# Graph-network kernel on one core: the last two pairs of edge blocks, with dst rows spread earlier and their output vectors in other PSUM banks

## The reference

```python
h = maximum(layernorm(x), 0)                              # 12500 x 32
e = concatenate([h[src], h[dst], edge_attr], axis=-1)     # 400000 x 96
v = relu(e @ W1 + b1) @ W2 + b2                           # 96 -> 64 -> 32
out = x + maximum(segment_max(v, dst), h)
```

## Time and profile before

| | us |
|---|---|
| median of three runs | 3227.99 |
| lowest, highest | 3225.35, 3228.82 |
| the profiled execution, its own time | 3226.88 |
| its span in the trace | 3224.7 |
| TensorE busy | 3004.2 |
| GpSimd busy | 2415.8 |
| VectorE busy | 2190.4 |
| ScalarE busy | 2111.5 |

### The profile page before, as it was taken

The page is one execution under the profiler, slowest core; times in us unless marked ns, Lnnn a source line. Parts: engine busy times, 40 slices in busy tenths (PEclk is TensorE's granted clock), DMA queues, the critical chain, the costliest instruction groups (busy, mean ns, idle before and its releaser), DMA issues.

```text
span 3224.7 us, 56108 instructions
## 1 busy us (share of the span) xinstructions
PE 3004.2 (93%) x19600; PEld 2220.3 (69%) x19600; DVE 2190.4 (68%) x2400; ACT 2111.5 (65%) x2463; POOL 2415.8 (75%) x2547
## 2 busy tenths in 40 slices
PE   6999999999999999999999999999998998999910
PEld 4776677777777777777777777777776776777700
DVE  6221677777777777777777777777776776777643
ACT  2335677777777777777777777777776775777510
POOL 7777777777777777777777777777777777777756
PEclk9999999999999999999999999999999999999955
DMA  9930333333333333333333333333333323333221
GB/s 310 362 128 27 84 101 101 100 99 99 95 98 98 100 96 102 100 98 95 97 99 98 100 97 101 101 98 85 106 98 90 100 77 102 101 99 98 75 47 26
DMA packets 194363, 337.83 MB, mean 105 GB/s; under 512 B 74115, under 2 KB 118101, under 8 KB 193712
## 3 DMA queue, kind: packets, MB, share of 16 engines
q1 hardware_dynamic: 110520, 292.58, 26.5%
q0 software_dynamic: 81216, 41.73, 10.1%
q10 hardware_dynamic: 2482, 2.14, 0.2%
HBM read 227.85 MB, written 108.41 MB: 104 GB/s over the span
## 4 chain that ended last, share of the span: by engine, by line
PE 89%; POOL 3%; issue 3%; DMA 3%; DVE 2%; SPq 0%; ACT 0%; DVEq 0%; POOLq 0%; ACTq 0%
PE ps_rows L734 67%; PE ps_layers L713 4%; PE ps_layers L715 4%; PE ps_layers L748 3%; PE ps_layers L763 3%; PE ps_layers L772 3%; PE ps_layers L752 3%; POOL gathered_max L597 2%; PE ps_layers L758 2%; DMA picks<-picks_dram 1%; POOL src_in L524 1%; DVE onehot L969 1%; DMA gathered_max<-run_max,gather_ix 1%; DMA src_in<-h_dram,src_ix 0%; DMA dst_i<-in_dst_dram 0%
## 5 line engine op out<-in xcount | busy, mean ns | idle before, releaser
L524 POOL DMA_INDIRECT src_in<-h_dram,src_ix x2293 | 2166.4, 945 | 698.8 <-issue 635.4
L734 PE MATMUL ps_rows<-onehot,table 128*128 128x512 f32 x9800 | 2288.7, 393 | 22.1 <-DVE onehot L969 22.1
L734 PEld LDWEIGHTS ps_rows<-onehot,table 128*128 128x128 f32 x9800 | 1830.0, 188 | 496.6 <-issue 107.3
L665 ACT ACTIVATE onehot<-distance 128x1024 fp32r<-128x1024 bf16 x882 | 878.9, 1049 | 701.2 <-PE ps_rows L734 701.2
L660 ACT ACTIVATE distance<-picks,below_column 128x1024 bf16<-128x1024 int16 x882 | 954.7, 1136 | 36.8 <-DMA picks<-picks_dram 36.8
L969 DVE SCALAR_TENSOR_TENSOR onehot<-picks,column,ps_layers 128x1024 fp32r<-128x1024 int16 x392 | 493.0, 1278 | 365.3 <-PE ps_rows L734 345.9
L713 PE MATMUL ps_layers<-ea_t,rows_in 125*128 125x320 bf16 x980 | 269.0, 302 | 25.4 <-DVE rows_in L838 25.4
L1015 DVE STREAM_TRANSPOSE ps_layers<-rows_in 128x512 f32<-128x512 f32 x196 | 129.4, 705 | 221.2 <-ACT hid L651 191.5
L715 PE MATMUL ps_layers<-dst_t,rows_in 125*128 125x320 bf16 x980 | 268.9, 301 | 0.0
L651 ACT ACTIVATE hid<-ps_layers,b_col 128x512 f32<-128x512 f32 x392 | 234.1, 674 | 37.7 <-PE ps_layers L763 37.7
L1030 DVE TENSOR_TENSOR_SCAN max_t<-mask_in,max_t,ps_layers 128x512 f32<-128x512 bf16 x196 | 250.4, 1278 | 9.0 <-PE ps_layers L772 5.5
(11 more groups left out here) (106 smaller groups left out, 1049.3 us busy)
## 6 DMA issues: line engine op xcount, KB each, us to landing
picks<-picks_dram SPq DMA_DIRECT2D x98, 512.0 KB, 11.0
first_rows<-hid SPq DMA_DIRECT2D x100, 500.0 KB
rows_in<-in_edge_attr_dram SPq DMA_DIRECT2D x97, 512.0 KB
rows_in<-first_rows SPq DMA_DIRECT2D x97, 512.0 KB
run_max<-rows_in SPq DMA_DIRECT2D x96, 512.0 KB
src_in<-h_dram,src_ix POOLq DMA_INDIRECT x2293
mask_in<-mask_dram SPq DMA_DIRECT2D x97, 256.0 KB
h_dram<-h_sb ACTq DMA_DIRECT2D x1, 1568.0 KB, 6.6
```

The source lines that it names most:

```text
L524: pool.indirect_dma_start(out=src_in[:, slot, g, r, :], out_offset=None, in_=rows[:, :], in_offset=bass.IndirectOffsetOnAxis(ap=src_ix[:, ...
L665: nc.scalar.activation(onehot[:, RING_AT[c] + BY_DVE[c] + k, :, :].rearrange("p g w -> p (g w)"), distance[:, k, :], ACT.Relu, bias=1.0, s ...
L734: mm = nc.tensor.matmul(ps_rows[g][side][:, 0:WIDE], table[:, i * SIDES + side, part, :], onehot[:, RING_AT[c] + t, g, :], start=(i + part ...
```

## The change

- `turn_edges` is cut in two: the turn of the attributes stays, the spread of the destination rows becomes `fill_dst`. In the pairs ahead of the end both stand one behind the other, as before. `fill_dst` has one more wait, for `dst_filled` at twice the pair's number.
- In pair 95 VectorE runs `fill_dst` for pair 97 too, ahead of the turn of pair 96's source rows.
- Layer one of pair 96 waits for the destination rows of both last pairs. Layer one of pair 97 no longer waits for the maxima of 96.
- Layer two of pair 96 writes to `ps_rows[0]` and that of pair 97 to `ps_rows[1]`, each once pair 97's picks have been masked.
- VectorE's last part is written out: attributes of 97, picks of 97, source rows of 97, maxima of 96, maxima of 97. The second scan of pair 97 covers 160 columns in place of 512.

The diff, cut to its core:

```diff
             def layer_one(j, slot, ahead, last):
-                wait(pe, max_scanned, j * 2)
+                wait(pe, max_scanned, j * 2 - 2 if last else j * 2)
...
-                pe.wait_ge(dst_filled, j * 2 + 2)
+                pe.wait_ge(dst_filled, j * 2 + 2 if ahead else PAIRS * 2)
...
-            def layer_two(j):
+            def layer_two(j, v=ps_v, looked_up=False):
+                if looked_up:
+                    pe.wait_ge(rows_masked, PAIRS * MASKS)
...
             for slot in range(2):
-                pair(PAIRS - 2 + slot, slot, ahead=False, last=slot == 1)
+                layer_one(PAIRS - 2 + slot, slot, False, slot == 1)
+                layer_two(PAIRS - 2 + slot, ps_rows[slot], True)
...
+            def fill_dst(j, slot, turn, through, last=False):
                 dve.wait_ge(first_loaded[slot], turn * D + (A * D if last else D))
                 dve.wait_ge(mask_loaded[slot], turn * D + D)
-                wait(dve, hid_made, j * A)
+                wait(dve, hid_made, through * A)
+                wait(dve, dst_filled, j * 2)
...
-            def find_max(j, slot, turn, again):
+            def find_max(j, slot, turn, again, v=ps_v, columns=BLK):
...
+                    n = columns if g else BLK
...
+                one_hot(j + 2, slot, 3)
+                find_side(j + 2, slot)
+                if before_last:
+                    dve.wait_ge(onehot_made, PAIRS * DVE_ALL)
+                    dve.wait_ge(side_found, PAIRS)
+                    fill_dst(j + 2, slot, of_slot + 1, j + 1, last=True)
+                turn_src(j + 1, (k + 1) % (2 * AHEAD), turn + (k + 1) // (2 * AHEAD))
...
+            turn_edges(PAIRS - 1, 1, PAIRS // 2 - 1, last=True)
+            mask_rows(PAIRS - 1, 1)
+            turn_src(PAIRS - 1, 2 * AHEAD - 1, DOUBLE_TURNS - 1, last=True)
+            find_max(PAIRS - 2, 0, PAIRS // 2 - 1, True, ps_rows[0])
+            find_max(PAIRS - 1, 1, PAIRS // 2 - 1, True, ps_rows[1], LAST - BLK)
```

More of the change, by code:

```diff
@@ L771, in layer_two, with pair @@
                     for a in range(A):
-                        mm = nc.tensor.matmul(ps_v[g][chunk(a), :], w_out[g * HID:(g + 1) * HID, :], hid[g * HID:(g + 1) * HID, a, :],
+                        mm = nc.tensor.matmul(v[g][chunk(a), :], w_out[g * HID:(g + 1) * HID, :], hid[g * HID:(g + 1) * HID, a, :],
                                               start=True, stop=True)
                 mm.then_inc(v_summed, 1)
[L776 to L779, removed]
+            def pair(j, slot):
+                layer_one(j, slot, True, False)
+                look_up(j + 2, slot, 0)
                 layer_two(j)
-                if ahead:
-                    for c in range(1, CHUNKS):
-                        look_up(j + 2, slot, c)
+                for c in range(1, CHUNKS):
+                    look_up(j + 2, slot, c)
             for j in range(2):
@@ L1028, in find_max @@
                 for g in range(2):
+                    n = columns if g else BLK
                     wait(dve, max_scanned, j * 2 + g)
[L1030 removed]
+                    V.tensor_tensor_scan(max_t[:, g, 0:n], mask_in[:, slot, g, 0:n], v[g][:, 0:n], max_t[:, 1 - g, BLK - 1:BLK],
                                          ALU.min, ALU.max).then_inc(max_scanned, 1)
@@ L1077, in _, with pair @@
             turn_edges(0, 0, 0)
-            def pair(j, k, turn, again, ahead=True, following=True, last_next=False):
+            fill_dst(0, 0, 0, 0)
+            def pair(j, k, turn, again, before_last=False):
                 slot = k % 2
                 of_slot = turn * AHEAD + k // 2
[L1083 to L1090, removed]
-                find_max(j, slot, of_slot, again)
[L1092 to L1097, removed]
+                dve.wait_ge(picks_loaded[slot], of_slot * D + 2 * D)
+                one_hot(j + 2, slot, 0)
+                mask_rows(j + 1, 1 - slot)
+                turn_edges(j + 1, 1 - slot, of_slot + slot)
+                fill_dst(j + 1, 1 - slot, of_slot + slot, j + 1)
+                one_hot(j + 2, slot, 2)
+                find_max(j, slot, of_slot, again)
+                one_hot(j + 2, slot, 3)
[5 more added lines that the diff above has]
+                turn_src(j + 1, (k + 1) % (2 * AHEAD), turn + (k + 1) // (2 * AHEAD))
             DOUBLE_TURNS = PAIRS // (2 * AHEAD)
```

3 lines of the change are left out of this document (2 added, 1 removed).

## The result

The changed kernel takes 3223.65 us (median of 22 runs, 3220.4 to 3225.86), the kernel before 3228.02 us (22 runs beside them, 3225.2 to 3234.46). The ratio is 0.9984, with a 95% interval of 0.9978 to 0.9990. By the medians that is 4.4 us less. By the means (3228.11 and 3223.02 us) it is 5.1 us, which is what the ratio stands for, with 3.2 to 7.1 us as its interval. The change is clear of zero, but smaller than the 0.2% that the text above calls the bound of what can be told. Forecast were 3221.3 us, 6.7 less, in a range of 3219.3 to 3225.5.

A forecast was written before the change was run, and what follows sets the result against it. TensorE and VectorE passing work back and forth over the last two pairs bound the end. Last turns moving from 3088.73 to 3082.06 gave 6.67 us less, so 3227.99 became 3221.3 us, range 3219.3 to 3225.5.

The forecast's parts named there:

- the 0.2% that the text above calls the bound of what can be told: Whole kernel: a measurement can tell about 0.2% from no change, 6.5 us, so the line for faster stood at 3221.5.
- The greater chance, 0.55: Whole kernel: chance given to faster, a time under 3221.5 us; same had 0.42 and slower 0.03.
- its own signs of being wrong: Changed trace: layer one of 96 moves, the gather wait is 4 us, or the early pairs change their pace.
- D: Mask ahead of both last pairs: a mask 17.1 us late makes the kernel 6 us slower, 3234; chance 0.03.
- E: Layer two of 96: something read as free, picks or bank change, holds it; no gain, 3228; chance 0.03.
- the landing of the last gather: Source rows of 97: landing at 3072.95, 3.9 us after issue, making TensorE about 1.0 us later than without it.
- rival B: Last gather as slow as pair 95's, 8.09 us, landing at 3077.1; 2.5 us less, 3225.5; chance 0.15.
- the 0.2 us for the semaphore: Last gather: 0.2 us estimated and added after the DMA traffic up to 3072.75, giving a landing at 3072.95.
- Rival C: TensorE's clock falls in pair 97: up to 2.5 us more, so 4.2 us less, 3223.8; chance 0.04.
- Rival A: Last gather lands by 3072, TensorE runs through pair 97, turns end at 3081.1; 7.6 us less, 3220.4; chance 0.22.

The follow-up runs named there:

- the run with TensorE kept busy: Changed kernel with two more matmuls, result written over, between layer one and layer two of each of the last two pairs; 3220.04 us, ratio 0.9981.
- the second run with the store held: Repeat of the changed kernel with pair 94's store and all SyncE does behind it held until pair 95's source rows landed; ratio 0.9976, kernels near 4340 us.
- the dst rows alone: Changed kernel with banks, order of source rows and maxima, and short scan undone; only pair 97's dst rows spread a pair sooner; 3224.29 us, ratio 0.9992.
- The control on the kernel before: Kernel before, with the input loaded again only once the last source gather has landed; ratio 1.0023, where every kernel took 4340 to 4380 us.

## Why the prediction was right or wrong

The time lay inside the range and the sign was right. The sum, 6.7 us, was 2.3 us too large by the medians, 1.6 by the means. The greater chance, 0.55, stood on a time under 3221.5, and that did not come. By its own signs of being wrong the prediction failed on two: layer one of 96 moved, and VectorE waited 7.00 us for the gather. The final gathers began at 3090.19 and not at 3086.6. That the time is in the range is partly luck: its upper end stood for a slower gather alone, while more than half of the 3.6 us by which the profiled execution missed its forecast (3085.69 against 3082.06) came with a start 2.24 us later, for which the sum had no term.

*What held.* Dst rows of 97 were spread in cover of the look-ups, without a wait for the mask. Source rows of 96, attributes and picks behind them were in time: layer one of 96 had no wait. Layer one of 97 followed layer two of 96 at once. The tail kept its 4.41 us. GpSimd's pace didn't change, the last gather was issued at 3069.01, and a pair still took TensorE 27.7 us. Rivals D and E did not come.

*The term that was too small: the landing of the last gather.* I read it from the windows of one execution as 3.9 us after the issue, and argued against rival B that "the windows show this very gather, under this very load". They showed it for one position of the load. The load begins when the look-ups end, and that date moved by 2.24 us against GpSimd's. The wanted rows were turned 6.8 us after the last issue instead of 3.9. The load's date explains 2.24 of the 2.9 us; the other 0.6 us is the 0.2 us for the semaphore, which no row showed: here 0.8 us or more lie between the last DMA traffic (over by 3075.00) and the turn (3075.80). The rows of the first block came no sooner, so their turn of 0.7 us stood behind the wait too, which the sum had left out. The landing follows how long the load was under way at the last issue: 7.8 us in the run with TensorE kept busy, and the turn came 2.6 us after the issue; 4.0 us with the loads of 97 held, 5.7 us; 2.9 us here, 6.8 us. Doubling the load cost 4.3 us, with intervals that are apart. Holding it gave 2.7 us back by the medians, 1.7 by the means. That the load holds up this gather and that this costs time is thus shown; how much, within a microsecond or so, is not. It lies between the forecast and rival B.

*The step that I held for unlikely: the clock.* Rival C had a chance of 0.04. I argued that TensorE would be busy in that stretch, so that the clock would stay. It fell at 3071.7, just as TensorE went back to work after 1.97 us, and in the same place when the input load was held. The two steps took 1.96 + 1.88 - 1.09 - 1.11 = 1.6 us more. In that execution this alone cost nothing, since the source rows were turned only by 3076.68. With the load held it did: the source matmuls came 10.06 us behind layer one of 96, and 8.41 us with TensorE kept busy as well. Where layer one of 97 follows at once and the two matmuls are not added, the clock fell at this gap in three profiled executions (the changed kernel, the load held, the store held) and stayed in three (the load doubled, the loads of 97 held, the second run with the store held); with the matmuls it stayed in all four. That is few, and what the edit is worth in time is not settled.

*Worked out for the two profiled executions.* Rival A, no wait for the gather, ended at 3081.1. Add 2.24 us for the later layer one of 96, 2.13 for the late source rows (1.64 of them spent at the lower clock, 0.49 waiting) and 0.12 for the scan (1.86 us for 1.74): 3085.6. Measured were 3085.69. So against a kernel before with the same late start the change would be worth some 5.3 us, and 3.0 remain because the profiled one of after had its layers later from pair 94 on.

*What stays open* is the last gather of pair 95, which sets that start. It let VectorE wait 6.36 us in the profiled execution before, 6.66 in that of after, not at all in that with the dst rows alone. Holding the loads of 97 did not cure it. The store of pair 94 is the likelier cause. In the seven profiled executions near 3220 us in which SyncE issued it ahead of this gather (by 0.15 to 2.1 us), the rows were turned 8.1 to 10.4 us after the gather's issue; in the three in which it came after, within 6.2 us. With the loads held it was 9.2 us in both executions, so those loads are not needed for it. This is an order read from traces: no run here removed the store, since the runs for it fell where no gather is late. The control on the kernel before fell there too, so that the load had no price ahead of the change is argued from its trace (source rows turned at 3077.8, all traffic over by 3072.75) and not shown by a run.

## What to carry to other kernels

When a wait is taken from one chain, look for transfers whose date doesn't move with it, and ask what the same edit starts beside them: here the chain ended at gathers that a bulk load, released by the end of the look-ups, held up. A landing read from one execution is one draw; where the other transfer hangs on another engine's date, keep both ends in the sum. Where two delays run beside one another, taking one away shows little until the other goes too. And where TensorE has idle gaps of some 2 us between short bursts, count its next steps at the lower clock as one end of the range; work that is thrown away in the gap is worth a try.

## What the runs showed of the hardware

- While SyncE's load ran in packets of 12.5 KB at 314 GB/s, GpSimd's gather queue moved no packet for 3 us (0 of 75). The Trainium skill (DMA: Bandwidth & Descriptors, Issuing engines are not separate DMA queues) says that transfers interleave whoever issues them; this stretch shows none of it. A stretch of another run does: with the load doubled, 85 gather packets moved beside 87 of SyncE's from 3069 to 3073.
- With that load out of the way, the last gather of 128 rows was there about 2.5 us after its issue; with it beside, the rows were turned after 6.8 us in the changed kernel; with twice as much, after 8.1 us. The same load, begun 7.8 us ahead of that gather, left it at 2.6 us.
- TensorE's granted clock fell to 0.50 while TensorE worked, after idle time of 1.97 us; in other executions the same idle time left it at 1.00. With two matmuls of no use in the gap it stayed at 1.00 in four executions of four.
- A masked scan over 160 columns made two scans take 1.86 us together, against 2.60 for two whole ones, so the short one costs about 0.57 us and not the 0.40 of its share.
